# Encoder: the tile's input is transposed by VectorE and DMA, and the first query product of the next tile stands in front of the Wo product

## What is computed

```python
for l in range(N_LAYERS):                                  # 6
    q = x @ Wq[l] + bq[l]; k = x @ Wk[l] + bk[l]; v = x @ Wv[l] + bv[l]
    a = causal_linear_attn(elu(q) + 1, elu(k) + 1, v)
    x = layer_norm(x + a @ Wo[l] + bo[l], g1[l], be1[l])
    y = gelu(x @ W1[l] + b1[l]) @ W2[l] + b2[l]
    x = layer_norm(x + y, g2[l], be2[l])
```

## Time and profile before

| | |
|---|---|
| time, median of 3 runs | 1638.76 us (1637.71 to 1641.25) |
| the profiled execution | 1638.76 us |
| its span, first to last instruction | 1637.0 us |
| mean granted TensorE clock | 0.986 of 2.4 GHz |
| busy: PE, DVE, ACT, POOL | 1550.9, 1259.2, 957.3, 785.4 us |
| DMA | 70.42 MB, mean 43 GB/s |

### The profile page before, as it was taken

One profiled execution on the slowest core, in us unless ns is written; L12 is line 12 of the kernel. 1 busy time (PEld: TensorE's weight loads), 2 busy tenths in 40 slices (PEclk: granted clock), 3 DMA queues, 4 the chain that ended last, 5 costly groups with the idle time before them and its releaser, 6 DMA issues.

```text
span 1637.0 us, 38440 instructions
## 1 busy us (share of the span) xinstructions
PE 1550.9 (95%) x16078; PEld 1242.9 (76%) x16078; DVE 1259.2 (77%) x2543; ACT 957.3 (58%) x1516; POOL 785.4 (48%) x580
## 2 busy tenths in 40 slices
PE   4799999999999999999999999999998999999798
PEld 3688888888888888888888888888887566666334
DVE  4767787877887877977879778788777888888456
ACT  3465556665566655655655556655534777777345
POOL 3354445545355453553545435553365466763334
PEclk8899999999999999999999999999999999999999
DMA  5100100100001000010000110001014444442001
GB/s 126 53 1 2 34 11 27 33 2 34 12 27 33 6 30 11 28 33 34 2 12 27 34 33 8 5 27 36 1 40 123 141 149 135 140 137 66 15 1 52
DMA packets 68908, 70.42 MB, mean 43 GB/s; under 512 B 17152, under 2 KB 56960, under 8 KB 68736
## 3 DMA queue, kind: packets, MB, share of 16 engines
q1 hardware_dynamic: 68736, 67.97, 14.0%
HBM read 50.78 MB, written 14.68 MB: 40 GB/s over the span
## 4 chain that ended last, share of the span: by engine, by line
PE 79%; DVE 13%; ACT 4%; issue 3%; SPq 1%; DMA 0%; POOL 0%; ACTq 0%; DVEq 0%
PE e_pr L167 9%; PE e_pr L169 7%; PE e_pr L168 7%; PE e_tr L414 6%; PE e_sc L387 5%; PE x_psO L1330 4%; PE e_sc L167 3%; PE e_sc L168 3%; PE e_sc L169 3%; PE e_tr L167 3%; PE e_tr L169 3%; PE e_tr L168 3%; PE e_tr L424 3%; PE f_bank L1868 2%; PE x_psT L1315 2%
## 5 line engine op out<-in xcount | busy, mean ns | idle before, releaser
L698 POOL TENSOR_TENSOR e_h_lo<-e_h_f,e_h_hi 128x512 fp32r<-128x512 f32 x192 | 247.2, 1290 | 303.5 <-ACT e_h_hi L540 300.8
L539 ACT ACTIVATE e_h_f<-e_pr,e_h_bias 128x512 f32<-128x512 f32 x192 | 132.0, 688 | 185.2 <-PE e_pr L169 181.5
L788 DVE TENSOR_TENSOR e_am<-e_sc,c_amask 128x1024 f32<-128x1024 f32 x192 | 225.7, 1216 | 18.1 <-PE e_sc L387 18.1
L1640 DVE TENSOR_REDUCE x_mx<-x_psS 128x4 f32<-128x1024 f32 x128 | 150.9, 1219 | 24.3 <-PE x_psS L1293 23.4
L167 PE MATMUL e_pr<-e_yT_hi,e_W_hi 128*128 128x512 f32 x384 | 168.7, 439 | 0.0
L167 PE MATMUL e_tr<-e_W_hi,e_h_hi 128*128 128x256 f32 x576 | 163.1, 283 | 0.0
L168 PE MATMUL e_tr<-e_W_lo,e_h_hi 128*128 128x256 f32 x576 | 160.9, 279 | 0.0
L169 PE MATMUL e_tr<-e_W_hi,e_h_lo 128*128 128x256 f32 x576 | 160.7, 279 | 0.0
L169 PE MATMUL e_pr<-e_yT_hi,e_W_lo 128*128 128x512 f32 x384 | 152.8, 398 | 0.0
L168 PE MATMUL e_pr<-e_yT_lo,e_W_hi 128*128 128x512 f32 x384 | 152.0, 396 | 0.0
L1466 ACT ACTIVATE x_ex<-x_psT 128x1024 f32<-128x1024 f32 x128 | 130.9, 1023 | 26.4 <-PE x_psT L1315 21.5
(11 more groups left out here) (281 smaller groups left out, 4341.8 us busy)
## 6 DMA issues: line engine op xcount, KB each, us to landing
e_raw_m<-in_L_attn_W_dram SPq DMA_DIRECT2D x12, 1024.0 KB, 7.2
x_qs<-query_rows SPq DMA_DIRECT2D x48, 256.0 KB
x_ks<-key_rows SPq DMA_DIRECT2D x48, 128.0 KB, 2.7
query_rows<-x_q_hi SPq DMA_DIRECT2D x16, 256.0 KB, 2.1
query_rows<-x_q_lo SPq DMA_DIRECT2D x16, 256.0 KB, 2.3
x_ctok<-in_ctx_dram SPq DMA_DIRECT2D x8, 256.0 KB, 3.4
x_xo<-in_x_dram SPq DMA_DIRECT2D x8, 256.0 KB, 3.8
key_rows<-x_k_hi SPq DMA_DIRECT2D x8, 256.0 KB, 2.2
```

The source lines that it names most:

```text
L539: act.activation(h_f[:, m % HR, :], ps_pr[m % 2][:, :], ACT.Gelu, bias=h_bias[:, m:m + 1])
L698: pool.tensor_tensor(h_lo[:, m, :], h_f[:, m % HR, :], h_hi[:, m, :].bitcast(F32), ALU.subtract).then_inc(h_lo_done, 1)
L788: dve.tensor_tensor(am[:, s % 2, c, :, :, :], ps_sc[:, :, c * 2 * P:(c + 1) * 2 * P].rearrange("p r (h n) -> p r h n", n=P), amask[:, :].u ...
L1640: dve.tensor_reduce(mx[:, N % 2, :, 0:HG].rearrange("p i (a h) -> p h a i", a=2)[:, pair], ps_s[pair][:, :, :].rearrange("p a (i j) -> p a ...
```

## The change

The transposes of the next tile's input leave TensorE. VectorE transposes the tile in one instruction, in 32x32 blocks, from `X` into `x_blocks`, which is the memory of `a_tok`. SyncE then moves the 16 combinations of block row and block column with 16 DMAs into `x_raw`, so that the whole is the transpose. ScalarE and VectorE make `xT_hi` and `xT_lo` from `x_raw` (SBUF) and no longer from PSUM. The instruction stands in VectorE's queue after the scaling and in front of `vx`; `x_hi` stands behind gelu(3) and gelu(4), `x_lo` in front of `aT_lo`. `divide(0)` now waits for the DMAs, since it writes into the memory that they read. On TensorE `qk(0)` of the next tile moves from the start of a step to the end of the step before, between `mlp_up(7)` and Wo. SyncE's loads are sorted into the steps, with the moves of each tile in front of them. In step -1 the first tile is still transposed by TensorE, and `qk(0)` stays where it was.

```diff
+    x_raw = sb_att("x_raw", [KC, TT])
+    x_blocks = a_tok[:, :, :].rearrange("p s d -> p (s d)").rearrange("p (c j n) -> p c j n", c=KC, j=NR)
+    MOVED = 16 * NR * NR
...
 SyncE
+            def move_x(t):
+                wait(sp, xT_lo_done, 2 * t)
+                wait(sp, x_moved, MOVED * (t - 1))
+                sp.wait_ge(xT_tr, t + 2)
+                for i in range(NR):
+                    for j in range(NR):
+                        sp.dma_start(x_raw[j * RH:(j + 1) * RH, :, blk(i)], x_blocks[i * RH:(i + 1) * RH, :, j, :]).then_inc(x_moved, 16)
+
+            def step(l, q, u, attn, mlp, following):
+                more = l < L - 1
+                if l > 0 and q == 1:
+                    sp.wait_ge(ln_done[2], SB * NT * l)
+                    load_rows(l, ["g2", "be2"], rows_m, ln2_rows_loaded)
+                if following:
+                    move_x(u + 2)
+                if q < 0:
+                    sp.wait_ge(w1_lo, 1)
+                    load_w2(0)
+                if more and q == 0:
...
+                    sp.wait_ge(w2_lo, l + 1)
+                    load_w1(l + 1)
...
 TensorE
-                def x_transpose(t, tile):
-
-                    for c in range(KC):
-                        wait(pe, aT_lo_done, 2 * (t - 1) + c + 1)
-                        for s in range(SB):
-                            mm = pe.transpose(ps_tr[c][:, blk(s)], X[:, tile * SB + s, blk(c)], ident[:, :])
-                        mm.then_inc(xT_tr, 1)
...
-                    for j in range(KC):
-                        if prev:
-                            pe.wait_ge(gelu_done, FC * u - 1 + j)
-                        elif mlp and j == 0:
-                            pe.wait_ge(ktok_done, t)
-                        qk(j)
+                    if u <= 0:
+                        wait(pe, ktok_done, t)
+                        qk(0)
+                    if prev:
+                        pe.wait_ge(gelu_done, FC * u)
+                    qk(1)
...
-                if following:
-                    if q < 0:
-                        pe.wait_ge(rest_loaded, 16 * (1 + FC))
-                    x_transpose(t + 1, (q + 2) % NT)
+                if following and mlp:
+                    pe.wait_ge(qkv_lo, (t + 1) // NT + 1)
+                    pe.wait_ge(xT_lo_done, 2 * t + 4)
+                    pe.wait_ge(gelu_done, FC * u + FC - 1)
+                    qk(0)
...
 ScalarE
+                def x_hi(t, c):
+                    act.wait_ge(x_moved, MOVED * t)
+                    act.activation(xT_hi[:, c, :].rearrange("p (s i n) -> p s i n", s=SB, i=NR),
+                                   x_raw[:, c, :].rearrange("p (i s n) -> p s i n", i=NR, s=SB), ACT.Copy).then_inc(xT_hi_done, 1)
...
+                    if following and s in (1, 2):
+                        x_hi(t + 1, s - 1)
...
-                if following:
-                    x_hi(t + 1)
...
 GpSimd
-                    add_row((q + 2) % NT, rows_a["bo"], xT_tr, 2 * t + 4, bo_loaded, 16 * (ln + 1), xbo_done)
+                    add_row((q + 2) % NT, rows_a["bo"], xT_tr, t + 3, bo_loaded, 16 * (ln + 1), xbo_done)
...
 VectorE
+                    if s == 0 and following:
+                        dve.wait_ge(x_moved, MOVED * (t + 1))
                     dve.tensor_tensor(a_tok[:, s, :].rearrange("p (h d) -> p h d", d=DH), o[:, :, 0:DH],
...
+                def x_transpose(t, tile):
+                    if t < NT:
+                        dve.wait_ge(rest_loaded, 16 * (1 + FC))
+                    else:
+                        dve.wait_ge(ln_done[2], SB * (t - NT) + SB)
+                    dve.transpose(x_blocks.rearrange("p c j (s n) -> p s (c j) n", s=SB),
+                                  X[:, tile * SB:(tile + 1) * SB, :].rearrange("p s (j n) -> p s j n", n=RH)).then_inc(xT_tr, 1)
+
                 def x_lo(t):
                     for c in range(KC):
                         dve.wait_ge(xT_hi_done, 2 * t + c + 1)
+                        dve.tensor_tensor(xT_lo[:, c, :].rearrange("p (s i n) -> p s i n", s=SB, i=NR),
+                                          x_raw[:, c, :].rearrange("p (i s n) -> p s i n", i=NR, s=SB),
+                                          xT_hi[:, c, :].bitcast(F32).rearrange("p (s i n) -> p s i n", s=SB, i=NR),
+                                          ALU.subtract).then_inc(xT_lo_done, 1)
...
                 if mlp:
                     scale(1, u, q, rows_a["be1"])
+                if following:
+                    x_transpose(t + 1, (q + 2) % NT)
...
+                if following:
+                    x_lo(t + 1)
                 if attn:
                     for c in range(KC):
                         dve.wait_ge(aT_hi_done, 2 * t + c + 1)
                         low(aT_lo[:, c, :], ps_tr[c][:, :], aT_hi[:, c, :]).then_inc(aT_lo_done, 1)
...
-                if following:
-                    x_lo(t + 1)
```

More of the change, by code:

```diff
@@ L142, in encoder @@
     kv_done, am_done, a_done, aT_lo_done = sem("kv_done"), sem("am_done"), sem("a_done"), sem("aT_lo_done")
-    den_done, rden_done = sem("den_done"), sem("rden_done")
+    den_step, x_moved = sem("den_step"), sem("x_moved")
     yT_lo_done = sem("yT_lo_done")
@@ L239, in _ @@
-            inputs.load(sp)
+            def move_x(t):
[16 more added lines that the diff above has]
+                if more and q == 0:
+                    sp.wait_ge(qkv_lo, l + 1)
+                    load_attn_weights(l + 1, ["Wq", "Wk", "Wv"], raw_qkv_loaded)
+                    sp.wait_ge(o_lo, l + 1)
+                    load_attn_weights(l + 1, ["Wo"], raw_o_loaded)
+                    sp.wait_ge(w2_lo, l + 1)
+                    load_w1(l + 1)
+                if more and q == NT - 2:
+                    sp.wait_ge(vx_done, 2 * (NT * l + NT))
+                    load_rows(l + 1, ["bv"], rows_a, bv_loaded)
+                    sp.wait_ge(xbo_done, NT * l + NT)
+                    load_rows(l + 1, ["bo"], rows_a, bo_loaded)
+                if more and q == NT - 1:
+                    sp.wait_ge(ln_done[1], SB * (NT * l + NT))
+                    load_rows(l + 1, ["g1", "be1"], rows_a, ln1_rows_loaded)
+                    sp.wait_ge(xb2_done, NT * l + NT)
+                    load_rows(l + 1, ["b2"], rows_m, b2_loaded)
+                    sp.wait_ge(w1_lo, l + 2)
+                    load_w2(l + 1)
+                if l == L - 1 and q == 1:
+                    inputs.load(sp)
@@ L240, in _ @@
+            steps(step)
             sp.wait_ge(o_lo, L)
@@ L276, in step @@
                     pe.wait_ge(x0_loaded, 16)
-                    x_transpose(0, 0)
+                    for c in range(KC):
+                        for s in range(SB):
+                            mm = pe.transpose(ps_tr[c][:, blk(s)], X[:, s, blk(c)], ident[:, :])
+                        mm.then_inc(xT_tr, 1)
                 def qk(j):
@@ L509, in step @@
                 more = l < L - 1
-                def x_hi(t):
+                def x_hi(t, c):
+                    act.wait_ge(x_moved, MOVED * t)
+                    act.activation(xT_hi[:, c, :].rearrange("p (s i n) -> p s i n", s=SB, i=NR),
+                                   x_raw[:, c, :].rearrange("p (i s n) -> p s i n", i=NR, s=SB), ACT.Copy).then_inc(xT_hi_done, 1)
+                if q < 0:
                     for c in range(KC):
-                        act.wait_ge(xT_tr, 2 * t + c + 1)
+                        act.wait_ge(xT_tr, c + 1)
                         act.activation(xT_hi[:, c, :], ps_tr[c][:, :], ACT.Copy).then_inc(xT_hi_done, 1)
-                if q < 0:
-                    x_hi(0)
                 def negative(j):
@@ L809, in x_lo @@
                         dve.wait_ge(xT_hi_done, 2 * t + c + 1)
+                        dve.tensor_tensor(xT_lo[:, c, :].rearrange("p (s i n) -> p s i n", s=SB, i=NR),
+                                          x_raw[:, c, :].rearrange("p (i s n) -> p s i n", i=NR, s=SB),
+                                          xT_hi[:, c, :].bitcast(F32).rearrange("p (s i n) -> p s i n", s=SB, i=NR),
+                                          ALU.subtract).then_inc(xT_lo_done, 1)
+                if q < 0:
+                    for c in range(KC):
+                        dve.wait_ge(xT_hi_done, c + 1)
                         low(xT_lo[:, c, :], ps_tr[c][:, :], xT_hi[:, c, :]).then_inc(xT_lo_done, 1)
-                if q < 0:
-                    x_lo(0)
                 last = (q - 1) % NT
```

34 lines of the change are left out of this document (5 added, 29 removed).

## The result

The kernel with the change takes **1619.76 us** (median of 4 runs, 1618.84 to 1621.31), the kernel before beside it 1639.39 us (1637.71 to 1641.25, 4 runs). The ratio is **0.9881**, 95% interval 0.9864 to 0.9898: 1.2% faster. The profiled execution took 1621.31 us, with a span of 1619.6 us and 1.7 outside; the profiled one before was 1638.76 with 1637.0. One of the four runs of the kernel of experiment 6 was slow (2717.51 us at a granted clock of 0.842) and is left out there.

What follows compares the result with a forecast made beforehand. TensorE was taken to bound the kernel, holding 79% of the chain. The terms -32.6 + 9.2 + 3.8 - 1.1 + 1.0 gave -19.7 us from 1638.8, so 1619 us, with a low end of 1611 and a high end of 1635.

Steps and rivals of the forecast that it cites:

- term 1: TensorE at 22 step ends: qk(0) fills the gap the transposes leave, -1.48 us each, -32.6 us.
- term 2: VectorE's new transpose of 128x1024 f32: 1.2 us, taken from the mask, with bounds 0.6 and 2.4.
- rival A: VectorE's transpose takes 2.4 us, so the kernel takes 1635 us; chance 0.12.
- term 3: VectorE at step starts: 2.0 us of slack hides the transpose in 17 ordinary starts; five with W1_lo give back 9.2 us.
- The five starts: Steps 4, 8, 12, 16, 20, with W1_lo: no VectorE slack, line 347 moves +0.35 us instead of -1.48, +9.2 us.
- term 4: Second half of a step: x_hi 0.6 us each on ScalarE, x_lo 0.9 x 2 on VectorE; no cost.
- rival B: x_lo slow beside GpSimd, so Wo waits 0.5 us for aT_lo at each end, 1630 us; chance 0.15.
- term 5: SyncE's queue: 16 DMAs at 0.58 us an issue, eight us of cover before divide(0) and x_hi; no cost.
- rival C: DMAs come late: at 1.2 us an issue the blocks are 1.7 us late, 1656 us; chance 0.08.
- term 6: Start-up: +3.8 us from VectorE's stall on the h_bias loads, -1.1 at Wo, +1.0 in step 0.
- Behind the last `yT`: Stretch from the last yT transposes to the end of the kernel: forecast change 0.
- the loop: Stretch from second to last yT: 21 ends at -1.48 us plus 9.2 for the five starts, -21.9 us.

Runs made afterwards that it cites:

- experiment 6: Changed kernel with the h_bias loads counted on another semaphore, so VectorE's first transpose does not wait for them: 1617.68 us, ratio 0.9881.
- Experiment 1: Changed kernel with qk(0) put back at the start of the step, transposes still on VectorE: 1641.78 us, ratio 1.0025.
- experiment 2: Changed kernel with VectorE's transpose made twice for each tile: 1633.36 us, ratio 0.997.
- Experiment 3: Changed kernel, W1_lo of layers 1 to 5 cut to 8 columns: 1609.84 us; transpose in five steps behind residual(2,0): 1617.48 us, behind residual(2,2): 1619.74 us.
- the kernel behind residual(2,2): Changed kernel with VectorE's transpose moved behind residual(2,2) in the five steps after a layer's last tile: 1619.74 us, ratio 0.988.
- experiment 5: Changed kernel with the blocks moved by 32 DMAs of 16 KB instead of 16 of 32 KB: 1726.36 us, ratio 1.0543.
- experiment 7: Changed kernel with W1_lo later and h_bias counted separately: 1616.04 us; also transpose behind residual(2,2) in five steps: 1621.83 us; changed kernel unaltered: 1619.62 us.

## Why the prediction was right

Forecast 1619 us, measured 1619.76; the medians lie 19.6 us apart (1639.39 and 1619.76), the two profiled executions 17.4, and the forecast said 19.7. Step by step:

- **The step ends** (term 1, -1.48 each): right in cause, a little small. An ordinary step is 1.54 us shorter. Experiment 1 shows that it is the filled gap, and that the cover carries it: without `qk(0)` in it, Wo does wait for `aT_lo`, 0.99 us, and had `aT_lo` come more than 0.35 us later, part of the gain would have gone. The cover was put at 0.4 us and is 0.35.
- **The transpose** (term 2): 1.24 us against 1.2, so the mask of the same size was the right row, and rival A is out. (Two of A's terms don't come out of its own inputs: 2.4 - 0.85 + 1.48 is 3.03 and not 3.06, and 2.4 - 2.0 is 0.4 and not 0.43. That is 0.7 us of its sum.) The Trainium skill, page "VectorE: DVE Perf Modes", section "The three transpose paths", gives the bf16 figure that I took eight times, for an estimate of 2.5 us; the trace does not agree with that estimate, and has no transpose of 128x128 to hold against the figure itself. The fault is in the scaling: rows of this kernel don't grow so either, 0.42 us for a residual of 256 columns and 1.18 for a mask of 1024. The page's advice to use TensorE for such a block leaves out what TensorE is to the kernel: here TensorE bounds the step.
- **The ordinary starts** (term 3): nothing, as forecast. The slack was put at 2.0 us, and experiment 2 hides 2.48 us in it, with 0.61 us of idle time left ahead of residual(2,2). One thing that I had not counted gives 0.75 us back: the transpose pushes `qx_lo` out from beside GpSimd's `k_lo`, 2.73 us against 3.48. So 1.73 us of the slack were used and 0.61 are left, 2.3 us in all: the slack was a little larger than I had put it.
- **The five starts**: +0.36 us each measured, +0.35 forecast. But the step of the argument that names the place failed. I had TensorE waiting some 1.8 us ahead of the `yT` transposes. It waits 1.61 us ahead of `mlp_down(2)`, for residual(2,0), and 0.21 ahead of `yT`. Experiment 3 shows how near the two chains are: once the transpose is out of the first, the second waits. The centring also grew, from 3.81 to 4.86 us, as VectorE now reaches it 1.23 us behind the start of `W1_lo` and not 2.49; my sum had no such term, so the agreement to 0.01 us is not as good as it looks.
- **`x_lo`** (term 4): the price was wrong, and that it cost nothing was luck: it hangs on an order that I had not looked at. I had read 0.87 us each for `qx_lo` as the price where little runs beside it; it is the mean of one at 1.49, beside `k_lo`, and three at 0.74. The pair of `x_lo` takes 2.37 us and not 1.8 (0.68 and 1.77). It ends at 597.59, where `aT_lo` starts, so rival B's wait did not come. But where `h_lo` starts first both are slow: 3.42 us, and TensorE waits 0.73 us in front of `qk(0)` (experiment 3). In step 12 of the change `x_lo` is ahead by 0.02 us, in step 11 by 0.07. `x_hi` was right at 0.62.
- **SyncE** (term 5): 0.67 us an issue, not 0.58. The last issue is over at 622.53; with 2.7 us of landing behind it, as in the prediction, the blocks would lie at about 625.2, against 632.01 for the division: 6.8 us of cover, not 8, and 5.3 in step 12 (663.87 + 10.58 + 2.7 to 682.40). The trace of the change has no landing for these DMAs. In that of the kernel behind residual(2,2) the median is 1.9 us from issue to landing (3.4 at most in step 20), which would make the cover over a microsecond longer in most steps. Experiments 3 and 5 show that rival C's mechanism is real once the cover is gone.
- **The start-up** (term 6, +3.7 in all): +4.9, as the second `yT` is 3.4 us later in spite of 1.48 gained at one end. The stall was 5.00 us and not 3.9, and Wo at the end of step -1 came 1.6 later instead of 1.1 earlier. At the end of step 0 both `x_lo` are slow and TensorE waits 0.65 us in front of `qk(0)`, for which the sum had no term. I had taken the start-up for a fixed sum; experiment 7 shows a spread of 7.6 us between executions, so the agreement here is partly luck.
- **Behind the last `yT`**: forecast nothing, +2.2 us. The kernels of this study show 414.2 to 417.3 us there, with the same code after the encoder, so I put this down to spread and not to the change. In two stretches of 20 us there, from 40 and from 300 us behind the last `yT`, the granted clock is 0.86 and 0.83 in the profile before, 0.75 and 0.74 in that of the change. What makes it was not tried.

The total was met because the loop was right to 1.1 us (-23.0 against -21.9) and start-up and end were too small by 3.4 together, which one profile can't tell from spread; the median of the four runs lies 1.5 us below the profiled one.

## What to carry to other kernels

Work taken off the bounding engine gives little while the wait that it covered stays: look for work that is ready and can stand in the gap, and count both parts together (here 0.34 + 1.20 us a step). An instruction given to a neighbour costs nothing up to that engine's idle time before its next deadline, so count it step by step, and take the steps where a third engine slows it down by themselves. Before moving such an instruction later, ask what its DMAs hold up, and what stands behind them in the queue: issued 6.3 us later, they cost 3.9 us in the worst of five steps, and with a weight load behind them 1.7 and 1.8 us in two others of another kernel. And look at instructions one by one: a mean of 1.19 us hid one of 0.68 and one of 1.77.
